# Pairs of heads with the second layer's projections spread evenly; the first layer's scores over all 128 rows from eight masked query variants

## The reference, cut to what matters

```
# layer 0: 16 heads of 16
q, k, v = query @ Wq + bq, key_value @ Wk + bk, key_value @ Wv + bv
attn = softmax(clip(q k^T * scale, -1e4, 1e4))        # per batch and head: 112 x 375
x = (attn v) @ Wo + bo
# layer 1: 16 heads of 64; the last 4 context tokens (ipa) have their own weights and softmax
q_in = x @ Wq + lora(x);  k_in, v_in = org_ctx @ Wk + lora, org_ctx @ Wv + lora
out = attention(q_in, k_in, v_in) + attention(q_in, ipa_ctx @ Wk_ipa, ipa_ctx @ Wv_ipa)
return out @ Wo + bo + lora(out)
```

## Time and profile before

| | |
|---|---|
| median of 3 runs | 1277.67 us (1271.22 to 1278.12) |
| profiled execution | span 1277.4 us |
| layer 0's attention | about 38 to 297 us; a batch takes 30.6 to 31.7 us |
| layer 1's attention | about 622 to 993 us; a batch takes 44.3 us |

### The profile page before, as it was taken

The page is one execution under the profiler, slowest core; times in us unless marked ns, Lnnn a source line. Parts: engine busy times, 40 slices in busy tenths (PEclk is TensorE's granted clock), DMA queues, the critical chain, the costliest instruction groups (busy, mean ns, idle before and its releaser), DMA issues.

```text
span 1277.4 us, 23029 instructions
## 1 busy us (share of the span) xinstructions
PE 1066.5 (83%) x7860; PEld 746.0 (58%) x7860; DVE 948.8 (74%) x2024; ACT 567.6 (44%) x1276; POOL 268.6 (21%) x303
## 2 busy tenths in 40 slices
PE   0688888882979999854688988998897699999997
PEld 0577777771634555643367877777776455455553
DVE  5588888897398888697567777777776667776775
ACT  3366666672433343441455556555555233222220
POOL 1422222202245563001000000000000013433331
PEclk9899999995699999896799999999998699999999
DMA  5000000001112122320000000000000231112100
GB/s 190 1 2 2 1 0 0 0 1 66 64 48 84 58 96 67 110 71 28 6 1 2 2 2 1 1 0 1 1 1 1 100 129 64 64 64 72 70 1 29
DMA packets 9935, 47.82 MB, mean 37 GB/s; under 512 B 1513, under 2 KB 3313, under 8 KB 6930
## 3 DMA queue, kind: packets, MB, share of 16 engines
q1 hardware_dynamic: 9874, 47.03, 10.7%
HBM read 45.92 MB, written 1.11 MB: 37 GB/s over the span
## 4 chain that ended last, share of the span: by engine, by line
PE 33%; DVE 30%; issue 20%; ACT 9%; POOL 5%; DMA 2%; DVEq 1%; ACTq 0%; POOLq 0%
PE pb L1119 8%; PE pb L1134 7%; POOL qz L1227 5%; DVE ST L844 4%; DVE ST L855 3%; DVE nm L850 3%; PE pb L640 2%; PE pb L613 2%; PE pb L597 2%; DVE ST L847 2%; ACT ST L728 2%; PE pb L1424 2%; PE pb L576 1%; ACT V L711 1%; PE pb L570 1%
## 5 line engine op out<-in xcount | busy, mean ns | idle before, releaser
L1119 PE MATMUL pb<-xT,KT 128*128 128x448 f16 x1248 | 244.2, 354 | 2.7 <-DVE qz L1197 2.7
L1227 POOL TENSOR_TENSOR qz<-qz,Z 128x448 f32<-128x448 f32 x128 | 169.1, 1331 | 286.8 <-ACT qz L1166 197.5
L1119 PEld LDWEIGHTS pb<-xT,KT 128*128 128x128 f16 x1248 | 121.6, 98 | 119.6 <-DVE qz L1197 5.8
L613 PE MATMUL pb<-KT,qz 128*112 128x375 f16 (+1 forms) x768 | 171.8, 334 | 3.2 <-POOL qz L921 2.1
L640 PE MATMUL pb<-V,ST 125*112 125x32 f16 (+1 forms) x1536 | 127.0, 214 | 53.2 <-DVE ST L855 52.9
L1134 PE MATMUL pb<-V,KT 128*128 128x448 f16 x816 | 162.6, 357 | 8.9 <-DVE V L1206 8.9
L640 PEld LDWEIGHTS pb<-V,ST 125*112 125x112 f16 x1536 | 109.9, 133 | 71.3 <-DVE ST L855 47.2
L736 ACT ACTIVATE ST<-pb 125x336 f16<-125x336 f32 x256 | 113.6, 444 | 45.1 <-PE pb L623 42.5
L855 DVE SCALAR_TENSOR_TENSOR ST<-pb,ST 125x336 f16<-125x336 f32 x256 | 127.7, 499 | 6.0 <-ACT ST L736 5.4
L1134 PEld LDWEIGHTS pb<-V,KT 128*128 128x128 f16 x816 | 80.3, 99 | 86.3 <-DVE V L1206 10.5
L623 PE MATMUL pb<-identf,ST 112*125 112x112 f32 x768 | 125.8, 273 | 1.6 <-ACT ST L728 1.6
(11 more groups left out here) (196 smaller groups left out, 1594.0 us busy)
## 6 DMA issues: line engine op xcount, KB each, us to landing
ST<-in_moe SPq DMA_DIRECT2D x9, 1536.0 KB, 7.8
ST<-in_moe SPq DMA_DIRECT2D x8, 1024.0 KB, 6.8
Z<-wd_scratch SPq DMA_DIRECT2D x16, 448.0 KB, 4.4
ST<-in_ctxT SPq DMA_DIRECT2D x4, 750.0 KB, 4.9
ST<-in_gens SPq DMA_DIRECT2D x2, 768.0 KB, 4.7
ST<-in_lora SPq DMA_DIRECT2D x2, 624.0 KB, 8.7
ST<-in_w1q SPq DMA_DIRECT2D x1, 1024.0 KB
ST<-in_w1k SPq DMA_DIRECT2D x1, 1024.0 KB
```

The lines of the kernel that those rows point to most:

```text
L613: mm = pe.matmul(SB_[st % 2][0:S, 0:L.keys], qz[:, bs % 2, qa, h, :], kT[bs % 2][qb][:, h // L.per_tile, 0:L.keys], start=(n == 0), stop=( ...
L1119: mm = pe.matmul(banks[m % len(banks)][:, 0:HT], MW[:, es % 2, qa, c:c + 128], xT[:, qb, k, half * HT:(half + 1) * HT], start=(i == 0), st ...
L1227: pool.tensor_tensor(tile, tile, wdB[:, es % 2, half * HT:(half + 1) * HT], ALU.mult)\
```

## The change

- Heads are taken in pairs. Scores of both heads fill both score banks; one `turn` has 6 transposes, one `hi` and one `lo` cover both heads (2x336 elements), and `weigh` has 12 matmuls. In layer 1 one maximum covers both heads. PE's order in step p is turn(p-1), units, weigh(p-2), units, scores(p+1). Scores(p+1) wait until both banks of pair p are read: by the clamps in layer 0, by the exponentials in layer 1.
- Layer 0: POOL's masks and `qu` are gone. The q unit writes eight variants of q instead, each scaled by a column of the mask (`par`), ACT the high parts and DVE the low parts, eight instructions each. The second clip moves from DVE to POOL.
- Layer 1: the scores of a pair use rows 0 to 63 for one head and rows 64 to 127 for the other, in turn. The units are spread by a new table. The division of `normalise` moves to POOL (`divide`), and the copy and addition become one reduction in both layers.

```diff
-NORM_LAG = (3, 3)
+NORM_LAG = 2
         if index == 0:
-            at = {0: 0, 1: 3, 2: 5, 3: 7, 4: 9, 5: 11}
-            out_at = {0: 5, 1: 8}
+            at = {0: 1, 1: 3, 2: 5, 3: 7, 4: 9, 5: 11}
+            out_at = {0: 5, 1: 13}
         else:
-            at = {n: min(15, n) for n in range(len(self.front))}
-            out_at = {0: 4, 1: 5, 2: 11}
+            at = dict(enumerate((1, 1, 2, 3, 3, 4, 5, 6, 7, 7, 8, 12, 13, 13, 14, 15, 15)))
+            out_at = {0: 5, 1: 9, 2: 11}
...
                 for n, (qa, qb) in enumerate(PARTS):
-                    mm = pe.matmul(SB_[st % 2][0:S, 0:L.keys], qz[:, bs % 2, qa, h, :],
-                                   kT[bs % 2][qb][:, h // L.per_tile, 0:L.keys], start=(n == 0), stop=(n == 2))
+                    for j, h in enumerate(L.pairs[p]):
+                        if l == 0:
+                            t, r = h // 8, slice(0, 128)
+                            q = qv[:, bs % 2, h % 8, qa, t, :]
+                        else:
+                            t, r = h // 2, slice(64 * (h % 2), 64 * (h % 2) + 64)
+                            q = qz[r, bs % 2, qa, h, :]
+                        mm = pe.matmul(SB_[j][0:S, 0:L.keys], q, kT[bs % 2][qb][r, t, 0:L.keys],
+                                       start=(n == 0), stop=(n == 2))
...
-                for h in range(H):
-                    scores(bv, bs, h)
...
+                for p in range(NP):
+                    if bs or p >= 1:
+                        turn(bv * NP + p - 1, bs * NP + p - 1)
...
+                    if p >= 2:
+                        weigh(bv, bs, p - 2)
...
+                    if p < NP - 1:
+                        scores(bv, bs, p + 1)
...
                 if u[0] == "q" and l == 0:
-                    act.activation(qu[:, bs % 2, 0, :, :], bank[:, 0:2 * S].rearrange("p (t n) -> p t n", t=2),
-                                   ACT.Copy, scale=QSCALE[0]).then_inc(g_hi, 1)
+                    for v in range(VAR):
+                        x = act.activation(qv[:, bs % 2, v, 0, :, :], bank[:, 0:2 * S].rearrange("p (t n) -> p t n", t=2),
+                                           ACT.Copy, scale=par[:, v:v + 1])
+                    x.then_inc(g_hi, 1)
...
-                    dve.wait_ge(s["mx_done0"], i + 1)
-                    dve.tensor_scalar(SC[:, st % 2, :], SC[:, st % 2, :], CLAMP, None, ALU.min)\
-                       .then_inc(s["clip_done0"], 1)
...
+                for i in range(B * NP):
+                    for j in range(2):
+                        pool.wait_ge(s["mx_done0"], 2 * i + j + 1)
+                        pool.tensor_scalar(SC[:, i % 2, j, :], SC[:, i % 2, j, :], CLAMP, None, ALU.min)\
+                            .then_inc(s["clip_done0"], 1)
...
+            def divide(bv, g):
+                group = bv * L.groups + g
+                heads = slice(g * L.grouped, (g + 1) * L.grouped)
+                ob = OB[:, g * 256:(g + 1) * 256].rearrange("p (h d) -> p h d", h=L.grouped)
+                pool.wait_ge(s["halves1"], group + 1)
+                pool.wait_ge(s["r_done1"], group + 1)
+                pool.tensor_tensor(ob, ob, bc(rinv[:, heads].unsqueeze(2), [S, L.grouped, L.dim]), ALU.mult)\
+                    .then_inc(s["o_rd1"], 1)
```

More of the change, by code:

```diff
@@ L615, in scores @@
                 mm.then_inc(s[f"s_mm{l}"], 1)
             def turn(i, st):
[L619 to L624, removed]
+                if l == 0:
+                    pe.wait_ge(s["exp_done0"], 2 * i + 2)
+                else:
+                    pe.wait_ge(s["ipa_patch1"], i + 1)
@@ L671, in attention_tensor @@
             batch("last", B - 1, B - 1)
[L672 to L675, removed]
+            turn(B * NP - 1, B * NP - 1)
+            weigh(B - 1, B - 1, NP - 2)
+            weigh(B - 1, B - 1, NP - 1)
             for _, kind, u, n, ns, _ in tail_units(L):
@@ L878, in batch @@
+                if l:
+                    return
+                dve.wait_ge(s["halves0"], group + 1)
+                dve.wait_ge(s["r_done0"], group + 1)
+                dve.tensor_tensor(ob, ob, bc(rinv[:, heads].unsqueeze(2), [S, L.grouped, L.dim]), ALU.mult)\
+                   .then_inc(s["o_rd0"], 1)
             def batch(where, bv, bs):
                 todo = unit_numbers(L, where, bv, bs)
[L880 to L896 removed]
@@ new lines, in batch @@
+                for p in range(NP):
+                    maxima(bv, bs, p)
+                    if bs or p >= 1:
+                        lo(bv * NP + p - 1, bs * NP + p - 1)
+                    for j in range(2):
+                        for hh, kind, u, n, ns, nh in todo:
+                            if hh == 2 * p + j:
+                                d = 1 if kind == "front" else -1
+                                unit(kind, u, n, ns, nh, bv + d, bs + d)
+                                if u[0] == "i":
+                                    ipa_rest(bv + d, bs + d)
+                        for g in range(L.groups) if j == 0 else ():
+                            at = (g + 1) * L.grouped // 2 - 1 + NORM_LAG
+                            if at == p:
+                                normalise(bv, bs, g)
+                            elif at == p + NP and bs:
+                                normalise(bv - 1, bs - 1, g)
@@ L907, in attention_vector @@
             batch("last", B - 1, B - 1)
-            for i in range(B * H - 2, B * H):
-                lo(i, i)
+            lo(B * NP - 1, B * NP - 1)
             normalise(B - 1, B - 1, L.groups - 1)
@@ L941, in patches @@
                         .then_inc(s["ipa_patch1"], 1)
+                    if bs and p == NORM_LAG - 1:
+                        divide(bv - 1, L.groups - 1)
+                    elif p > NORM_LAG and (p - NORM_LAG) % 2:
+                        divide(bv, (p - NORM_LAG - 1) // 2)
             patches(0, 0)
@@ L947, in attention_gpsimd @@
             patches(B - 1, B - 1)
+            divide(B - 1, L.groups - 1)
         def attention_sync(sp, L):
```

237 lines of the change are left out of this document (113 added, 124 removed).

## The result

The changed kernel takes 1328.85 us (median of 4, 1323.1 to 1332.13) against 1277.89 us: 1.0398 times as long [1.0355, 1.044]. It is slower by 51 us; the forecast was 31, the range 1258 to 1345. The profiled execution has a span of 1321.4 us against 1277.4, so 44 us is what the rows must explain (the profiled execution was the fastest of the four). That the time lies in the range is luck: one price was far too low, other terms of layer 0 and the waits of layer 1 were too dear, and the errors largely cancel.

A forecast was written before the change was run, and what follows sets the result against it. PE was taken to bound layer 1, and DVE's own work to set layer 0's pace. Layer 0 at +31 and layer 1 at 0 gave 1277.5 + 31 + 0 = 1309 us, range 1258 to 1345.

The forecast's parts named there:

- other terms of layer 0: Layer 0 batch: eight plain steps 25.0 us, PE's step longer by 0.6, units other than q 2.8.
- the waits of layer 1: PE's uncovered waits in a full layer-1 batch: together 4.4 us, so a batch takes 43.2 against 44.3.
- POOL's clip: Layer 0's second clip on POOL: 0.5 us, with slack in plain steps, counted in the step with a q unit.
- the q step: Layer 0's step with the q unit: lasts 8.2 us instead of 3.1, with nothing covering it.
- POOL's clip is slow: Rival, layer 0: clip 1.1 us instead of 0.5, two in series, +8 a batch, +64, 1373 us; chance 0.07.
- The q burst: Layer 0's q unit: eight instructions on ACT, 2.9 us, then eight on DVE, 3.1 us, not overlapping and uncovered.
- Half clock: Layer 0: PE's idle time lowers the granted clock; one turn, weigh and scores at half clock cost 1.5 us.
- The wait behind q: Layer 1, the step behind q: DVE frees the bank late, an uncovered wait of 1.2 us.
- the ipa step: Layer 1: scores(5) wait for an exponential behind the ipa chain, 1 us.
- the third unit of the other steps: Layer 1: a step's third unit needs the bank of the first, 0.3 to 0.5 us in four steps.
- in part: Rival, layer 1: the array packs in part, a batch of 40 us, -30, 1279 us, no change; chance 0.12.
- the even spreading: Layer 1's new table of units: in the full-packing rival it leaves only 1 us idle, 37.7 a batch; chance 0.20.

The follow-up runs named there:

- run 2: The change with layer 0's second clip left out, ACT reading the clamp's output directly: 1263.99 us, ratio 0.989.
- run 1: The change with layer 0's second clip back on DVE, POOL doing nothing in layer 0: 1286.58 us, ratio 1.0079.
- run 4: The change with four masked q variants instead of eight, half the heads reading another head's variant: 1304.5 us, ratio 1.0215.
- run 6: The change with layer 0's masks back on POOL and the second clip on DVE, leaving only the pairing there: 1267.08 us, ratio 0.9902.
- runs 7 and 9: Layer 1's old table of units put back, first in the kernel of run 5 (1253.08 us), then in the change (1316.18 us).
- run 5: Layer 0's attention of the kernel before, with layer 1's attention of the change: 1264.24 us, ratio 0.9896.

## Why the prediction was right, and where it was not

*Slower, by more than 0.5%:* right, and so were the kinds of terms. Three parts were mis-sized: the clip, the other terms of layer 0, and the waits of layer 1.

*POOL's clip: the step that failed.* I took 0.5 us "by the number of inputs"; it measured 1.147, above even the upper bound of 1.1. The rate of two inputs was near, and the row of 128 elements that I went by is another operation (in proportion it would give 0.86 us; the 0.5 needs a fixed part that the rows shown don't have). The sentence "in a plain step the clips have about 1 us of slack and cost nothing" held nearly: without a unit and at full clock the step is 3.0 to 3.2 us with POOL's clips and 2.9 without any. What failed is that the forecast put the clips into the q step alone. In a step with a v unit it had 3.12 + 0.2 = 3.3 us; without a clip such a step takes 2.90 (run 2), with DVE's 3.37 (run 1), with POOL's 4.27. The rival "POOL's clip is slow" had just this: two clips in series on the loop of the steps with a unit, about 1.3 us in each such step (measured 1.37 over no clip), and a price of +64. It had a chance of 0.07. Against no clip POOL's costs 65 us by the medians (1328.85 and 1263.99) and 63 by the ends of layer 0, where the forecast's sum had 0.65 a batch, about 5; against one on DVE it costs 42 by run 1. The Trainium skill, page "GPSIMD Engine Reference", section 4.1, calls one-input operations on GpSimd roughly line-rate, and by that sentence I had dismissed the rival. The trace does not agree: the clip takes 1.147 us on POOL and 0.31 on DVE (run 1), and its 3.06 ns an element are no less than the 2.4 of the two-input `divide` of 256 elements (614 ns).

*The q burst:* ACT 2.80 and DVE 2.96 us (forecast 2.9 and 3.1), in series and uncovered; run 4 confirms it at 24 us for half. Net of the masks, variants cost 20 us in layer 0.

*The other terms of layer 0:* too dear, by 3 to 4 us a batch. Without any clip (run 2) the seven batches average 30.8 us, where the sum, less its 0.65 for the clip, had 34.4. A plain step takes 2.9 us there and not 3.12, steps with a v unit 2.9 and not 3.3, and the q step 7.1 to 7.9 where the forecast had 8.2 with the clip. Layer 0 ends 3.5 us later in run 2 than before, where the forecast without its clip term had +26. This hid 23 us of the clip's price from the sum. Pairing alone costs 5 to 8 us by run 6, whose batches are mostly 31.1 us.

*Half clock:* the fall came, to 0.87 and 0.91 in the batches. The 1.5 us set for it are of the right size: run 2's batches of the same code take 30.1 to 30.3 us where the granted clock is 0.94 and 31.9 where it is 0.89.

*Layer 1, forecast 0, measured -22:* scores of a pair 0.61 us instead of 0.74 (full overlap, and one change of the rows' group at 0.28 us of the weight load's wait), so PE's work is 38.5 us against the 38.8 forecast, which is small. The wrong term is the waits: 4.4 us forecast, 2.3 there. The wait behind q came (1.38 us, forecast 1.2: DVE frees the bank late), and the ipa step waits 0.72 us (forecast 1). But the third unit of the other steps does not wait at all (forecast 1.6 in four steps), and the small ends are 0.2 (forecast 0.6). A batch at 40.8 is near the rival "in part" (40 us, -30); the last batch gave back less than the +8 set for it (its pairs step at 3.4 us, not 3.8). The Trainium skill, page "TensorEngine Tiling (Array Packing)", section Tiling Modes, lets different tiles run in parallel; the trace agrees, with 0.61 against 0.99 us from six matmuls to the next product, the 0.28 us wait of the next weight load included.

*The table:* I took the even spreading as part of what closes PE's gaps. It costs 0.8 us a batch (runs 7 and 9). In the windows half of it is PE's idle time (2.3 against 1.9 us: the wait for a k unit's bank is 0.9 us longer, the waits of the scores 0.6 shorter) and half its busy time (38.51 against 38.08), for which the rows give no cause.

So +31 came from +31 and 0, and the runs have +66 and -22. In the profiled execution's 44 us: 31 forecast, 58 more for the clip, 23 less for the other terms of layer 0, 22 less for layer 1. The time landed in the range because these cancel, not because the prices were right.

## What to carry to other kernels

A moved instruction costs what it costs on the new engine, and it sits wherever its consumers wait: before moving work off a busy engine to an idle one, close the loop through it in rows, for the steps with a unit as well as for the plain ones, and take its price from a row of the same operation, or from the dearest near one. In-order engines gain when a consumer has other work between it and its producer: pairing heads was worth more in layer 1 than packing the array. Judge each stage of a multi-part change by itself: here the layer-1 part with the old table is 2% faster than before, and the change as a whole 4% slower.

## What the runs showed of the hardware

POOL's one-input clip of float32 costs 2.5 to 3.1 ns an element, no less than its two-input operations (2.4 for the `divide` of 256 elements, 3.0 for 448 elements). Two groups of 64 rows in the array work side by side when the matmuls alternate between them, and the way back to 128 rows costs 0.28 us before the next weight load and 0.1 after it. The same batch of layer 1 took 40.6 to 40.8 us at a granted clock of 1.00 and 42.4 at 0.96, and such dips fell in different batches of kernels whose layer 1 is the same; 6.4 us of difference between two such kernels (351.6 us in run 5, 345.2 in the change) came with that alone.
